# Adding scatter transfers onto rows that hold x and half the shared expert, in a Macaron block

## The chip, the cores and the metric

One core of one Trainium2 chip runs the whole program in one launch. The metric is the device time of a run in microseconds, median of several runs. The engines are named as in the profile: PE (TensorE matmuls), PEld (its weight loads), DVE (VectorE), ACT (ScalarE), POOL (GpSimd), SP (SyncE, which only issues transfers here).

## The reference

Input x has 32 x 256 = 8192 tokens of 128 features, float32. The block is feed-forward, attention, feed-forward, each on a layer norm of x:

```
x = x + 0.5 * ffn(layernorm(x))
x = x + attention(layernorm(x))        # linear attention: phi(q) (phi(k)^T v) Wo^T + bo, 16 heads of 8, per batch of 256 tokens
x = x + 0.5 * ffn(layernorm(x))
ffn(h)  = shared(h) + sum over the 2 best of 8 routed experts of score_e * down_e(silu(gate_e h) * up_e h)
shared(h) = down(silu(gate h) * up h)  # inner width 256, for the shared and for each routed expert
```

The routing (sigmoid of logits, two best of eight, scores divided by their sum) depends on the data, so tokens are sorted by expert on the chip.

## The kernel before, in words

The tokens are 16 tiles of 512; x stays in SBUF as 16 slices of 128 x 512 (four tokens a partition). The order of the work is written out by hand for each engine, with semaphores between them. The program has five parts, where f is 0 for the first feed-forward and 1 for the second.

1. Dispatch (f = 0, to about 173 us). Per tile: layer norm into `send`, transpose, router, two best experts and a place in the expert's list for each pick (`route`, DVE), the shared expert (`gate_up`, `down_shared` on PE). DVE adds half the shared expert to x in `add_shared` (line 1342). POOL scatters each tile's normalised rows, with their number and weight, into `x_rows` in HBM: `ffn_tile` (line 639), 8 indirect transfers of 128 rows per tile.
2. Slot stage f = 0 (to about 367 us). 68 slots of 256 rows of one expert (three are mixed). SP loads the rows of a slot (`load_rows`, line 508, six slots ahead), PE transposes them, gate and up are made in three fp32r matmuls each, DVE multiplies (line 1781), PE makes the down product (line 1122), DVE scales it by the row's weight into a ring of 12 result buffers (`slot_results`, lines 1791 and 1793), and POOL scatters it to `y_rows` in HBM: `slot_tile` (line 651), 2 indirect transfers of 128 rows of 512 bytes per slot. Each token has two rows there, one per pick. When a tile's slots have been sent, SP loads its 512 KB back (`load_picks`, line 528, ring of two) and DVE adds both picks to x (`add_pick`, line 1686, twice) and takes the statistics of attention's norm (`norm_stats`). Eight tiles are added inside the stage, eight later.
3. Middle (16 turns and a few on either side, to about 580 us). Turn i does attention of tile i and, one and two turns behind, routing and the shared expert of f = 1. In `attend` PE first puts the output bias into the bank (line 1196: a matmul of two rows of ones by two rows that hold bo split in two parts), then adds the four products of phi(q) (line 1199). DVE adds the bank to x (line 1858). POOL scatters rows as in the dispatch.
4. Slot stage f = 1 (to about 759 us), as the first one, with stores of finished tiles (line 532) among the loads.
5. The last loads of results, additions and stores (to 778.5 us).

POOL's own order is: all of the dispatch's transfers, then those of the 68 slots, then the same again. Nothing else of weight is on it. SP issues in one order too: ahead of a slot stage the two tables of slots, the first six slots' rows, eight paddings (line 544), then row 6 on.

Of the kernel before, what the change touches and what calls it, by code (L numbers as in the profile page):

```python
# [13 lines left out]
P = 128  # L14
# [32 lines left out]
BY_VECTOR = (2, 3)  # L47
LATE_TURN = {t: t - LATE for t in range(LATE, TILES)}
# [58 lines left out]
def macaron(nc, x_in, w_experts, router_wT, routing_bias, w_attn, bq, bv, bo, out):  # L107
# [15 lines left out]
    with ExitStack() as ctx:  # L123
# [34 lines left out]
        bo_rows = sb("bo_rows", [2, P])  # L158
        bo_hi = sb("bo_hi", [2, P], F32R)
        bo_lo = sb("bo_lo", [2, P])  # L160
        bo_first = sb("bo_first", [2, P])
        bo_parts = sb("bo_parts", [2, P], F32R)
        ones_rows = sb("ones_rows", [2, P], F32R)
# [35 lines left out]
        y_pair = sb("y_pair", [P, 2, PICKS, TT])  # L199
        nobody_pad = y_pair.rearrange("p i w n -> p (i w n)")[:, 0:(PAD_BLOCKS - ROUTED) * JS * ROW].rearrange(  # L200
# [97 lines left out]
        bq_ready, ones_ready, bo_ready = sem("bq_ready"), sem("ones_ready"), sem("bo_ready")  # L298
# [14 lines left out]
        shared_psum, shared_added = sem("shared_psum"), sem("shared_added")  # L313
# [10 lines left out]
        first_added, both_added = sem("first_added"), sem("both_added")  # L324
# [140 lines left out]
        def _(sp):  # L465
# [14 lines left out]
            sp.dma_start(bo_rows[:], bo.partition_broadcast(2)).then_inc(attn_loaded, 16)  # L480

            for e in range(1, EXPERTS):
                wait_count(sp, split_lo, 0 if e == 1 else split_expert(e - 2))
                sp.dma_start(w_raw[e % 2][:], w_experts[e, :, 0:2 * INNER]).then_inc(w_loaded[e % 2], 16)
                if e == 2:
                    sp.wait_ge(pad_ready, 1)
                    sp.dma_start(x_rows[ROUTED * region:].rearrange("(b p j) d -> p b (j d)", p=P, j=JS),
                                 nobody_pad.rearrange("p b j d -> p b (j d)")).then_inc(nobody_region, 16)

# [31 lines left out]
            def load_picks(f, t):  # L521

                n = f * tiles + t
                wait_count(sp, both_added, n - Y_RING + 1)
# [5 lines left out]
            def store_tile(t):  # L530
                sp.wait_ge(both_added, tiles + t + 1)
                sp.dma_start(out_view[t], x[:, t, :].rearrange("p (b n) -> p b n", b=2)).then_inc(stored, 16)

            for f in range(2):
                load_tables(f, 0, FIRST_SLOTS)
# [35 lines left out]
                if f == 0:  # L571
                    for t in range(len(loads), tiles):
# [13 lines left out]
        def _(pool):  # L586
# [58 lines left out]
            def slot_tile(f, s):  # L645
# [17 lines left out]
        def _(act):  # L663
# [50 lines left out]

            def send_second(f, t):
# [18 lines left out]
            def dispatch():  # L734
# [19 lines left out]
                split_high(1)  # L754
                silu_tile(f, 2)
                send_normalised(f, 4)
                high((FFN, f, 4))
                send_normalised(f, 5)
                silu_tile(f, 3)
                send_normalised(f, 6)  # L760
# [8 lines left out]
                for b in range(WRITTEN_OUT, len(BATCHES[f])):  # L769
# [7 lines left out]
                    if len(ahead) > 1:  # L777
                        high((FFN, f, ahead[1]))
                    if len(ts) > 1:
                        for c in range(HALVES):  # L780
                            silu(f * tiles + ts[1], c)
                    for t in ts:
                        if 1 <= t < EXPERTS:
                            split_high(t)
                        if t == tiles - 3:
                            act.wait_ge(attn_loaded, 80)
                            act.activation(bo_hi[:], bo_rows[:], ACT.Copy).then_inc(bo_ready, 1)
                            act.wait_ge(ones_ready, 1)
                            act.activation(ones_rows[:], ones[0:2, :], ACT.Copy).then_inc(bo_ready, 1)
# [37 lines left out]
            def slot_stage(f):  # L827
# [3 lines left out]
                for s in range(slots):  # L831
# [7 lines left out]
                    slot_silu(f, s)  # L839
                    ahead = s - NORMALISE_FROM  # L840
# [40 lines left out]
            def middle():  # L881
                for i in range(TURNS.stop):
# [3 lines left out]
                    if i + 2 < tiles:  # L886
                        high((ATTN, 1, i + 2))
                    if proj:
# [32 lines left out]
        def _(pe):  # L921
# [83 lines left out]
            def down_shared(f, t):  # L1005
# [4 lines left out]
                wait_count(pe, shared_added, n)  # L1010
# [100 lines left out]
            def slot_down(f, s):  # L1111
# [6 lines left out]
                if s == 0:  # L1118
                    pe.wait_ge(shared_added, (f + 1) * tiles)
# [69 lines left out]
            def attend(t):  # L1189
# [3 lines left out]
                pe.wait_ge(shared_added, tiles + max(0, t - LAG_G - 1))  # L1193
                if t == 0:
                    pe.wait_ge(bo_ready, 5)
                pe.matmul(att_bank[:].rearrange("p (j d) -> p j d", j=SUB), ones_rows[:],
                          bo_parts[:].unsqueeze(1).to_broadcast([2, SUB, P]), start=True, stop=False)
                for j in range(SUB):
                    last = pe.matmul(att_bank[:, j * P:(j + 1) * P], phi_q[t % 2][:, j * P:(j + 1) * P],  # L1199
                                     kvo_sb[:, j // 2, :], start=False, stop=(j == SUB - 1))  # L1200
# [43 lines left out]
        def _(dve):  # L1244
# [3 lines left out]
            def norm_stats(item):  # L1248
# [8 lines left out]
                if kind == ATTN:  # L1257
                    dve.wait_ge(both_added, t + 1)
# [420 lines left out]
            def add_pick(f, t, w):  # L1679

                n = f * tiles + t
                if w == 0:
                    dve.wait_ge(y_loaded[t % Y_RING], (n // Y_RING + 1) * 16)
                else:
# [290 lines left out]
```

## Time and profile before

| | us |
|---|---|
| median of 3 runs | 778.35 |
| lowest and highest run | 770.6, 781.48 |
| the profiled execution | 780.31 |
| its span | 778.5 |
| busy: PE, PEld | 690.4, 612.7 |
| busy: DVE, ACT, POOL | 552.3, 469.2, 535.9 |

The span is what the trace covers; the execution's own time is 1.8 us longer. Times of rows count from the start of the span. The busy time of POOL counts the generation of a transfer, not the pause behind it; that of PE counts modelled ends of pipelined matmuls.

### The profile page before, as it was taken

The numbers are of one execution on the slowest core, as the hardware profiler recorded it, in microseconds if no ns is written. First come the engines' busy times: TensorE is split into PE (matmuls) and PEld (weight loads), VectorE is DVE, ScalarE is ACT, GpSimd is POOL, SyncE is SP. The second block draws the span as 40 slices with busy tenths as digits, with TensorE's granted clock in tenths as the row PEclk, the third lists the DMA queues.
The fourth block names the chain that finished last, engine by engine and source line by source line (L and its number), as shares of the span: only waits on it lengthen the run. The fifth ranks groups of instructions, "written<-read, shape, count | busy, mean of one in ns | idle before, by whom it ended". The sixth has DMA issues, their size and how long they took to land.

```text
span 778.5 us, 17599 instructions
## 1 busy us (share of the span) xinstructions
PE 690.4 (89%) x4981; PEld 612.7 (79%) x4981; DVE 552.3 (71%) x1858; ACT 469.2 (60%) x865; POOL 535.9 (69%) x567
## 2 busy tenths in 40 slices
PE   5586867969999999899799999999989999999990
PEld 4466766859999998888566777777769999999990
DVE  6686877886555557767778888877787555567772
ACT  3334534526766776676766767676446766777760
POOL 3474777777777777777257676767777777777773
PEclk8588867989999999999999999999999999999995
DMA  9313221143354345554213211111324354467765
GB/s 279 97 52 121 78 66 49 53 124 107 101 164 132 102 130 152 151 157 137 72 55 95 70 42 43 43 45 46 87 79 122 109 169 115 136 206 227 220 202 171
DMA packets 63445, 89.65 MB, mean 115 GB/s; under 512 B 13174, under 2 KB 43768, under 8 KB 63352
## 3 DMA queue, kind: packets, MB, share of 16 engines
q1 hardware_dynamic: 46456, 53.63, 24.3%
q0 software_dynamic: 16896, 34.90, 13.3%
q8 instruction: 44, 0.72, 0.4%
q14 instruction: 49, 0.40, 0.2%
HBM read 46.36 MB, written 42.12 MB: 114 GB/s over the span
## 4 chain that ended last, share of the span: by engine, by line
PE 61%; DVE 21%; DMA 6%; issue 5%; ACT 2%; SPq 2%; POOL 1%; POOLq 0%; DVEq 0%; ACTq 0%
PE y_bank L1122 12%; PE y_bank L1016 5%; PE g_bank L924 4%; DMA y_pair<-y_rows 4%; PE g_bank L926 4%; PE u_bank L925 4%; PE u_bank L924 4%; PE u_bank L926 4%; PE g_bank L925 4%; PE g_bank L995 3%; PE u_bank L996 3%; PE tr_bank L946 2%; DVE stats L1264 2%; DVE h L1337 2%; PE y_bank L1199 2%
## 5 line engine op out<-in xcount | busy, mean ns | idle before, releaser
L639 POOL DMA_INDIRECT x_rows<-send,send_to x256 | 248.8, 972 | 144.4 <-issue 67.5
L651 POOL DMA_INDIRECT y_rows<-send,y_to x272 | 265.0, 974 | 85.2 <-issue 66.2
L1781 DVE TENSOR_TENSOR h<-silu_g,u_bank 128x512 f32<-128x512 f32 x136 | 93.2, 685 | 110.8 <-ACT silu_g L825 109.2
L800 ACT ACTIVATE slot_gu<-w_gu 128x1024 fp32r x130 | 137.7, 1060 | 40.6 <-issue 36.9
L1122 PE MATMUL y_bank<-w_dn,h 128*128 x1088 | 143.6, 275 | 0.4 <-DVE x L1342 0.4
L1122 PEld LDWEIGHTS y_bank<-w_dn,h 128*128 128x128 f32 x1088 | 132.9, 191 | 0.9 <-issue 0.8
L924 PE MATMUL g_bank<-xT_hi,slot_gu 128*128 128x256 f32 x260 | 84.8, 326 | 14.4 <-DVE xT_lo L1772 13.5
L1016 PEld LDWEIGHTS y_bank<-w_dn,h 128*128 128x128 f32 x512 | 65.3, 202 | 26.9 <-issue 26.2
L825 ACT ACTIVATE silu_g<-g_bank 128x512 f32<-128x512 f32 x136 | 78.9, 580 | 9.7 <-PE g_bank L926 9.6
L1016 PE MATMUL y_bank<-w_dn,h 128*128 128x128 f32 x512 | 66.9, 287 | 16.6 <-DVE x L1342 16.6
L699 ACT ACTIVATE silu_g<-g_bank 128x512 f32<-128x512 f32 x64 | 38.0, 596 | 72.5 <-PE u_bank L926 41.4
L925 PE MATMUL u_bank<-xT_lo,slot_gu 128*128 128x256 f32 x260 | 73.0, 281 | 0.0
L924 PE MATMUL u_bank<-xT_hi,slot_gu 128*128 128x256 f32 x260 | 73.0, 281 | 0.0
L926 PE MATMUL u_bank<-xT_hi,slot_gu 128*128 128x256 f32 x260 | 73.0, 281 | 0.0
L925 PE MATMUL g_bank<-xT_lo,slot_gu 128*128 128x256 f32 x260 | 72.9, 280 | 0.0
L926 PE MATMUL g_bank<-xT_hi,slot_gu 128*128 128x256 f32 x260 | 72.8, 280 | 0.0
L924 PEld LDWEIGHTS g_bank<-xT_hi,slot_gu 128*128 128x128 f32 x260 | 49.2, 189 | 19.9 <-DVE xT_lo L1772 18.1
L1686 DVE TENSOR_TENSOR x<-y_pair,x 128x512 f32<-128x512 f32 x64 | 43.9, 685 | 23.2 <-DMA y_pair<-y_rows 23.0
L711 ACT ACTIVATE send<-x,shift,rstd 128x128 f32<-128x128 f32 x128 | 52.5, 482 | 10.0 <-DVE shift L1304 7.9
L1793 DVE TENSOR_TENSOR send<-y_bank,send 128x256 f32<-128x256 f32 x136 | 56.8, 418 | 0.6 <-PE y_bank L1122 0.3
L925 PEld LDWEIGHTS g_bank<-xT_lo,slot_gu 128*128 128x128 f32 x260 | 49.6, 191 | 0.0
L925 PEld LDWEIGHTS u_bank<-xT_lo,slot_gu 128*128 128x128 f32 x260 | 49.2, 189 | 0.0
(258 smaller groups left out, 1484.0 us busy)
## 6 DMA issues: line engine op xcount, KB each, us to landing
send<-x_rows SPq DMA_DIRECT2D x130, 130.0 KB
y_pair<-y_rows SPq DMA_DIRECT2D x32, 512.0 KB
y_rows<-send,y_to POOLq DMA_INDIRECT x272, 2.7
x<-x_in SPq DMA_DIRECT2D x16, 256.0 KB, 7.2
x_rows<-send,send_to POOLq DMA_INDIRECT x256
out<-x SPq DMA_DIRECT2D x16, 256.0 KB
w_raw<-w_experts SPq DMA_DIRECT2D x15, 256.0 KB, 4.0
x_rows<-pad SPq DMA_DIRECT2D x16, 130.0 KB
```

The lines of the kernel that those rows point to most:

```text
L639: pool.indirect_dma_start(x_rows, bass.IndirectOffsetOnAxis(ap=send_to[b % SEND_TO_RING][:, w, k:k + 1], axis=0), send[ring_of(f, t)][:, w ...
L651: pool.indirect_dma_start(y_rows, bass.IndirectOffsetOnAxis(ap=y_to[k][:, j:j + 1], axis=0), result_rows(f, s)[:, j, :], None).then_inc(y_ ...
L711: last = act.activation(send[ring_of(f, t)][:, 0, j, 0:P], x_sub(t, j), ACT.Identity, bias=bias, scale=scale)
L800: act.activation(slot_gu[n % 2][:].rearrange("p a n -> p (a n)"), w_gu[:, bass.ds(e, 1)].rearrange("p e a n -> p (e a n)").bitcast(F32), A ...
L825: act.activation(silu_g[n % 2][:], g_bank[n % 2][:], ACT.Silu).then_inc(slot_silu_done, 1)
L924: pe.matmul(bank_ap, w_parts[0], x_parts[0], start=True, stop=False)
L925: pe.matmul(bank_ap, w_parts[0], x_parts[1], start=False, stop=False)
L926: return pe.matmul(bank_ap, w_parts[1], x_parts[0], start=False, stop=True)
L1016: last = pe.matmul(shared_bank[:, s], h[t % 2][c][:, s], w_dn[:, 0, c, :], start=(c == 0), stop=(c == HALVES - 1))
L1122: last = pe.matmul(y_bank[par][:, j * P:(j + 1) * P], h[par][0][:, c * ROWS + j * P:c * ROWS + (j + 1) * P], w_dn[:, bass.ds(e[j % len(e)] ...
L1781: dve.tensor_tensor(h[par][0][:], silu_g[par][:], u_bank[par][:], ALU.mult).then_inc(slot_h_done, 1)
L1793: dve.tensor_tensor(result_rows(f, s), y_bank[n % 2][:, 0:ROWS].rearrange("p (j d) -> p j d", j=JS), row[:, :, WEIGHT:WEIGHT + 1].to_broad ...
```

## The change

Rows of `y_rows` are no longer overwritten by the slots' results but added to. Ahead of the slots SP stores x of each tile into the rows of its first pick and half the shared expert into those of its second (`store_base`, 32 tiles x 2 transfers of 256 KB). Half the shared expert comes from ACT, out of the PSUM bank into one of two new buffers (`shared_to_half`). The scatter of line 651 gets `compute_op=ALU.add`. When a tile comes back, x is the sum of the two loaded rows: one addition in place of two, and DVE's `add_shared` is gone. The padding rows of `y_rows` are cleared once. POOL waits, ahead of slot 0 of each stage, for all 16 tiles' stores. ACT waits, ahead of a half, for the stores of the tile two before it. Attention's output bias, broadcast over the partitions (`bo_b`), is added to x by DVE (`add_bias`) between `mask_heads` and `value`, and the bias matmul with its small preparation on ACT and DVE is gone. In the first slot stage attention's statistics are taken one slot earlier.

```diff
+HALVES_AFTER = {2: (0, 1, 2), 5: (3, 4), 7: (5, 6), 8: (7,)}
@@ sync
+            def store_base(f, t):
+                sp.wait_ge(shared_halved, f * tiles + t + 1)
+                sp.dma_start(y_tiles[t][:, 0, :], x_tile(t)).then_inc(base_stored[t % 2], 16)
+                sp.dma_start(y_tiles[t][:, 1, :], shared_half[t % 2][:]).then_inc(base_stored[t % 2], 16)
             for e in range(1, EXPERTS):
                 wait_count(sp, split_lo, 0 if e == 1 else split_expert(e - 2))
                 sp.dma_start(w_raw[e % 2][:], w_experts[e, :, 0:2 * INNER]).then_inc(w_loaded[e % 2], 16)
-                if e == 2:
+                if e == 3:
                     sp.wait_ge(pad_ready, 1)
...
+                for t in HALVES_AFTER.get(e, ()):
+                    store_base(0, t)
...
             for f in range(2):
+                for t in range(HALVES_AFTER[EXPERTS - 1][-1] + 1 if f == 0 else 0, ROWS_TILE + 2 + (f == 0)):
+                    if f == 1 and t == 1:
+                        load_picks(0, tiles - 1)
+                    store_base(f, t)
                 load_tables(f, 0, FIRST_SLOTS)
...
                 for s in range(ROW_RING):
                     load_rows(f, s)
+                for t in range(ROWS_TILE + 2 + (f == 0), tiles - 1):
+                    store_base(f, t)
                 sp.wait_ge(table_step, f * TABLE_STEPS + FIRST_STEPS + 1)
                 for e in range(ROUTED):
...
+                store_base(f, tiles - 1)
                 for s in range(ROW_RING, FIRST_SLOTS):
                     load_rows(f, s)
@@ gpsimd, slot_tile
                 pool.wait_ge(y_out_done, n + 1)
+                if s == 0:
+                    pool.wait_ge(nobody_cleared, 32)
+                    for done in base_stored:
+                        pool.wait_ge(done, (f + 1) * tiles * 16)
                 for j in range(JS):
                     pool.indirect_dma_start(
                         y_rows, bass.IndirectOffsetOnAxis(ap=y_to[k][:, j:j + 1], axis=0),
-                        result_rows(f, s)[:, j, :], None).then_inc(y_sent[k], 16)
+                        result_rows(f, s)[:, j, :], None, compute_op=ALU.add).then_inc(y_sent[k], 16)
@@ scalar
+            def shared_to_half(f, t):
+                n = f * tiles + t
+                act.wait_ge(shared_psum, n + 1)
+                wait_count(act, base_stored[t % 2], n // 2 * PICKS * 16)
+                act.activation(shared_half[t % 2][:], shared_bank[:], ACT.Copy, scale=0.5).then_inc(shared_halved, 1)
@@ tensor, attend
-                pe.matmul(att_bank[:].rearrange("p (j d) -> p j d", j=SUB), ones_rows[:],
-                          bo_parts[:].unsqueeze(1).to_broadcast([2, SUB, P]), start=True, stop=False)
@@ vector
-            def add_shared(f, t):
-                dve.wait_ge(shared_psum, f * tiles + t + 1)
-                dve.scalar_tensor_tensor(out=x_tile(t), in0=shared_bank[:], scalar=0.5, in1=x_tile(t), op0=ALU.mult,
-                                         op1=ALU.add).then_inc(shared_added, 1)
-                dve.tensor_tensor(x_tile(t), y_in[t % Y_RING][:, w, :], x_tile(t), ALU.add).then_inc((first_added, both_added)[w], 1)
+                dve.tensor_tensor(x_tile(t), y_in[t % Y_RING][:, 0, :], y_in[t % Y_RING][:, 1, :], ALU.add
+                                  ).then_inc(picks_added, 1)
+            def add_bias(t):
+                dve.wait_ge(xn_done, t + 1)
+                dve.tensor_tensor(by_sub(x_tile(t)), by_sub(x_tile(t)), bo_b[:].unsqueeze(1).to_broadcast([P, SUB, P]), ALU.add
+                                  ).then_inc(bias_added, 1)
```

On DVE, at the end of the dispatch, behind the routing of the last two tiles (`pad_table` is the last piece of it, `h` the shared expert's product, `x<-y_bank` is `add_shared`, `blocks` the start of the table of slots), the order before was:

```order
L1567 CAST pad_table<-filled 1x8
L1342 SCALAR_TENSOR_TENSOR x<-y_bank,x 128x512
L1337 TENSOR_TENSOR h_0<-silu_g,u_bank 128x512
L1337 TENSOR_TENSOR h_1<-silu_g,u_bank 128x512
L1342 SCALAR_TENSOR_TENSOR x<-y_bank,x 128x512
L1569 SCALAR_TENSOR_TENSOR blocks<-filled,counting 128x80
```

In the changed kernel the same place on DVE reads:

```order
L1591 CAST pad_table<-filled 1x8
L1366 TENSOR_TENSOR h_0<-silu_g,u_bank 128x512
L1366 TENSOR_TENSOR h_1<-silu_g,u_bank 128x512
L1593 SCALAR_TENSOR_TENSOR blocks<-filled,counting 128x80
L1598 SCALAR_TENSOR_TENSOR blocks<-filled,counting 128x8
```

Both additions are gone, so that the table follows the products at once.

On PE, in a turn of the middle, where `attend` follows the second half of the next tile's projection (`attn_raw,pad`) and comes ahead of the router, before:

```order
L1186 MATMUL y_bank<-attn_raw,kv_sb 128x128 x2
L946 MATMUL tr_bank<-ident,send 128x128 x4
L1163 MATMUL g_bank<-attn_raw,pad 128x256 x2
L1196 MATMUL y_bank<-bo_parts,ones_rows 128x512
L1199 MATMUL y_bank<-kvo_sb,phi_q 128x128 x4
L967 MATMUL route_bank<-router_raw,pad 128x8 x4
```

and in the changed kernel, on PE in the same turn:

```order
L979 MATMUL tr_bank<-ident,send 128x128 x4
L1196 MATMUL g_bank<-attn_raw,pad 128x256 x2
L1228 MATMUL y_bank<-kvo_sb,phi_q 128x128 x4
L1000 MATMUL route_bank<-router_raw,pad 128x8 x4
L1202 MATMUL u_bank<-pad,attn_raw 128x512
```

The matmul of the bias is gone from each of the 16 turns; the rest keeps its order.

On SP, where the eighth padding goes out ahead of the slot stage (`x_rows<-pad`) and the seventh slot's rows follow (`send<-x_rows`), before:

```order
L544 ISA
L544 DMA x_rows<-pad 128x260
L506 TENSOR_LOAD row_table
L506 ISA x2
L508 ISA
L508 DMA send<-x_rows 128x260
```

and in the changed kernel, on SP at the same place:

```order
L561 DMA x_rows<-pad 128x260
L483 DMA y_rows<-x 128x512
L484 DMA y_rows<-shared_half 128x512
L517 TENSOR_LOAD row_table
L517 ISA x2
L519 ISA
L519 DMA send<-x_rows 128x260
```

The last tile's two stores stand between the paddings and the rows of slot 6.

## Rows read from the trace of the kernel before

**Rows 1.** Busy time of the engines in four stretches, with clock and DMA share.

```profile
core 0: us, PE busy (x) PEld busy (x) DVE busy (x) ACT busy (x) POOL busy (x), PEclk, DMA share, GB/s
300.00:320.00 20.00, 17.76 (x146) 16.93 (x147) 14.01 (x37) 13.34 (x20) 15.15 (x16) 1.00 0.51 150
500.00:520.00 20.00, 20.00 (x124) 15.05 (x124) 16.07 (x65) 14.71 (x33) 14.69 (x16) 1.00 0.14 44
640.00:660.00 20.00, 20.00 (x179) 20.00 (x178) 10.57 (x28) 12.85 (x21) 15.12 (x17) 1.00 0.45 132
700.00:720.00 20.00, 20.00 (x175) 19.80 (x174) 14.87 (x39) 14.46 (x24) 15.38 (x16) 1.00 0.76 223
```

**Rows 2.** Lines 639 and 651: GpSimd's transfers, ns min/median/max, first and last start.

```profile
L639 POOL DMA_INDIRECT x_rows<-send,send_to x256: 952/964/1369, 23.5 to 590.0; - x128
L651 POOL DMA_INDIRECT y_rows<-send,y_to x272: 952/963/1482, 201.2 to 766.0; - x136
DMA to landing us min/median/max: 2.3/2.7/4.9
```

**Rows 3.** Timeline of GpSimd: start us, us, line, operation [idle before <- releaser].

```profile
77.54 0.97 POOL L639 DMA_INDIRECT x_rows<-send,send_to  x1 [9.03 <-DVE number_weight L1438]
...
201.25 0.96 POOL L651 DMA_INDIRECT y_rows<-send,y_to  x1 [0.30 <-DVE send L1793]
...
374.25 0.97 POOL L651 DMA_INDIRECT y_rows<-send,y_to  x1 [0.31 <-issue]
...
591.30 0.96 POOL L651 DMA_INDIRECT y_rows<-send,y_to  x1 [0.30 <-issue]
...
766.01 0.96 POOL L651 DMA_INDIRECT y_rows<-send,y_to  x1 [0.30 <-issue]
```

**Rows 4.** Timeline of TensorE in one turn of the middle.

```profile
445.76 1.03 PE L1163 MATMUL g_bank<-attn_raw,pad 128*128 128x256 f32 x4
446.72 0.49 PE L1196 MATMUL y_bank<-bo_parts,ones_rows 2*128 2x512 f32 x1
447.14 1.16 PE L1199 MATMUL y_bank<-kvo_sb,phi_q 128*128 128x128 f32 x8
```

**Rows 5.** Timeline of ScalarE in the same turn.

```profile
445.08 0.60 ACT L699 ACTIVATE silu_g<-g_bank 128x512 f32<-128x512 f32 x1 [0.87 <-PE u_bank L996]
```

**Rows 6.** Timeline of VectorE where the first slot stage begins.

```profile
168.09 0.69 DVE L1342 SCALAR_TENSOR_TENSOR x<-y_bank,x 128x512 f32<-128x512 f32 x1 [1.02 <-PE y_bank L1016]
...
173.42 0.42 DVE L1772 TENSOR_TENSOR xT_lo<-tr_bank,xT_hi 128x256 fp32r<-128x256 f32 x1
...
179.25 0.69 DVE L1342 SCALAR_TENSOR_TENSOR x<-y_bank,x 128x512 f32<-128x512 f32 x1 [1.64 <-PE y_bank L1016]
```

**Rows 7.** Timeline of TensorE where the first slot stage begins.

```profile
173.89 0.58 PE L924 MATMUL g_bank<-xT_hi,slot_gu 128*128 128x256 f32 x1 [5.40 <-DVE xT_lo L1772]
```

**Rows 8.** Timeline of SyncE's transfers ahead of both slot stages.

```profile
162.70 6.41 SPq L508 DMA_DIRECT2D send<-x_rows  x6
...
577.75 8.73 SPq L544 DMA_DIRECT2D x_rows<-pad  x8
```

**Rows 9.** Timeline of VectorE at one of stage 0's loads of results.

```profile
298.54 0.69 DVE L1686 TENSOR_TENSOR x<-y_pair,x 128x512 f32<-128x512 f32 x1 [1.77 <-DMA y_pair<-y_rows]
...
300.55 0.68 DVE L1686 TENSOR_TENSOR x<-y_pair,x 128x512 f32<-128x512 f32 x1
```

**Rows 10.** Waits from 280 to 366 us: us in total, times, longest.

```profile
DVE x L1686 <- DMA y_pair<-y_rows: 11.9, 8, 2.3
```

**Rows 11.** Timeline of VectorE at the end.

```profile
767.56 1.42 DVE L1686 TENSOR_TENSOR x<-y_pair,x 128x512 f32<-128x512 f32 x2 [7.01 <-DMA y_pair<-y_rows]
...
774.49 1.42 DVE L1686 TENSOR_TENSOR x<-y_pair,x 128x512 f32<-128x512 f32 x2 [0.33 <-DMA y_pair<-y_rows]
```

**Rows 12.** DMA queues: packets, MB, share of 16 engines.

```profile
q1 hardware_dynamic: 46456, 53.63, 24.3%
q0 software_dynamic: 16896, 34.90, 13.3%
```

More of the change, by code:

```diff
@@ L199, in macaron @@
         y_pair = sb("y_pair", [P, 2, PICKS, TT])
+        shared_half = two("shared_half", [P, TT])
         nobody_pad = y_pair.rearrange("p i w n -> p (i w n)")[:, 0:(PAD_BLOCKS - ROUTED) * JS * ROW].rearrange(
@@ L488, in _ @@
                                  nobody_pad.rearrange("p b j d -> p b (j d)")).then_inc(nobody_region, 16)
+                    for b, n in ((0, ROUTED), (ROUTED, PAD_BLOCKS - ROUTED)):
+                        sp.dma_start(y_rows[nobody + b * ROWS:nobody + (b + n) * ROWS].rearrange("(p k) d -> p k d", p=P),
+                                     pad.rearrange("p e j d -> p (e j) d")[:, 0:n * JS, 0:P]).then_inc(nobody_cleared, 16)
+                if e == 2:
+                    sp.wait_ge(x_rest, 16 * (tiles - 4))
+                for t in HALVES_AFTER.get(e, ()):
+                    store_base(0, t)
             def load_tables(f, first, last):
@@ L571, in _ @@
                 if f == 0:
-                    for t in range(len(loads), tiles):
+                    for t in range(len(loads), tiles - 1):
                         load_picks(f, t)
@@ L784, in dispatch @@
                             split_high(t)
[L785 to L789, printed above, removed]
                     if b + 2 < len(BATCHES[f]):
@@ L839, in slot_stage @@
                     slot_silu(f, s)
+                    if s == 0:
+                        shared_to_half(f, tiles - 1)
                     ahead = s - NORMALISE_FROM
@@ L887, in middle @@
                         high((ATTN, 1, i + 2))
+                    if 0 <= i - LAG_G - 2 < tiles - 1:
+                        shared_to_half(1, i - LAG_G - 2)
                     if proj:
@@ L1118, in slot_down @@
                 if s == 0:
-                    pe.wait_ge(shared_added, (f + 1) * tiles)
+                    pe.wait_ge(shared_halved, (f + 1) * tiles)
                 for j in range(JS):
@@ L1192, in attend @@
                 wait_count(pe, x_attended, t)
[L1193 to L1197 removed]
+                pe.wait_ge(shared_halved, tiles + max(0, t - LAG_G - 1))
                 for j in range(SUB):
                     last = pe.matmul(att_bank[:, j * P:(j + 1) * P], phi_q[t % 2][:, j * P:(j + 1) * P],
[L1200 removed]
+                                     kvo_sb[:, j // 2, :], start=True, stop=True)
                 last.then_inc(att_psum, 1)
@@ L1713, in dispatch @@
                 norm(3)
-                add_shared(f, 0)
                 multiply_tile(f, 2)
                 norm(4)
-                add_shared(f, 1)
                 low((FFN, f, 4))
@@ L1721, in dispatch @@
                 padding_constants()
-                add_shared(f, 2)
                 for t in range(1, 4):
@@ L1805, in slot_stage @@
                     table_piece(f, (s, THEN))
-                    if s == 0:
-                        add_shared(f, tiles - 1)
                     table_piece(f, (s, BEHIND))
@@ L1890, in middle @@
                         mask_heads(i)
+                        add_bias(i)
                     if 0 < i + 1 < tiles:
                         value(i + 1, 0)
-                    for t in late:
-                        add_pick(0, t, 0)
                     if g:
@@ L1928, in middle @@
                         route(1, i - LAG_T, MASK_STEP, RECIP_STEP)
-                    if 0 <= i - LAG_G - 1 < tiles - 1:
-                        add_shared(1, i - LAG_G - 1)
                     if g and i - LAG_G == tiles - 1:
@@ L1939, in _ @@
             for t in range(tiles):
-                for w in range(PICKS):
-                    if first_add(1, t) + w >= slots:
-                        add_pick(1, t, w)
+                if first_add(1, t) >= slots:
+                    add_picks(1, t)
 _OUT = ((32, 256, 128), "float32")
```

58 lines of the change are left out of this document (23 added, 35 removed).

## The prediction

> **What bounds the kernel now.** I read the windows first. In both slot stages PE is full or nearly so: 20.00 of 20 us at 640 and 700, 17.76 at 300; in the middle, at 500, it is 20.00 as well, with DVE at 16.07 and ACT at 14.71 [rows 1]. That looks like a PE kernel, and DVE's additions like work beside the path. But POOL shows 15.1 to 15.4 of 20 in every slot window, with 16 or 17 transfers, and that is a full engine too: a transfer takes 0.96 us and 0.30 us pass before the next [rows 2, 3], 1.26 us together, and 16 of them fill 20 us. From 77.54, after a wait of 9.03 us for DVE's routing, to 201.25 POOL makes 96 transfers of the dispatch (123.7 us, 1.29 each), from 201.25 to 374.25 the 136 of stage 0 (1.28 a pitch), and from 591.30 to 766.01 the 136 of stage 1 (1.29) [rows 3]. PE's 68 slots are done some 8 us earlier each time. So the end of the program hangs on POOL: last transfer at 766.01, 0.96 for it, landing 2.7 [rows 2], the last load of results, the last two pairs of additions from 774.49 on [rows 11], the last store. Stage 1 is POOL's from its first transfer on; in it nothing that DVE, ACT or PE saves can count, only what lets POOL start earlier or go faster. After stage 0 POOL has slack: it stands still from 375 until the middle has routed a tile, so stage 0 and the middle are paced by PE, with the waits of rows 6, 7 and 9.
>
> **The change part by part.** I sum against the profiled execution, 780.3 us; the median of the three runs, 778.35, is 2.0 below it.
>
> *The bias matmul goes (16 turns).* In a turn that is PE's from end to end the bias starts at 446.72 and the first product behind it at 447.14 [rows 4]: 0.42 us. 16 x 0.42 = 6.7 us off PE in the middle. Bounds: 16 x the matmul's own 0.49 = 7.9, and 0 if another engine takes the turn over. What comes in its place: an addition on DVE of the size of line 1342 (0.69 us [rows 6]), while add_shared (0.69) leaves each turn, and in the first eight turns one of two pick additions (0.68 [rows 9]) as well. DVE is not longer in any turn. ACT gets one copy of 128x512 out of PSUM, like the silu of 0.60 us [rows 5]; it stands just ahead of that silu, which waited 0.87 us for PE. It fits, with 0.3 us to spare. I take -6.7.
>
> *add_shared leaves the dispatch and the first slot.* The first slot's gate matmul starts at 173.89, after PE stood still for 5.40 us for DVE's xT_lo at 173.42 [rows 6, 7]. The slot's rows were asked for at 162.70 [rows 8], so that is about 5 us later than its input allows. DVE was late because it had two add_shared to do, the second after a wait of 1.02 us for PE, and then the table; and at 179.25 a third, after 1.64 us. Those alone are 0.69 + 1.02 + 0.69 + 1.64 + 0.69 = 4.7 us of DVE's row, and some more was saved in the pairs of tiles before. The row request itself waits for POOL's transfers of the dispatch and does not move. Bounds: 0 and the whole 5.4 + 1.6 + 0.7 = 7.7. I take -5.0.
>
> *POOL's start in the dispatch.* POOL's last gap is the 9.03 us until 77.54 [rows 3], for routing of tiles 4 and 5, and DVE has up to three add_shared less ahead of it; against that six stores now stand between SP's loads of the experts. Bounds +1 and -3 x 0.69 = -2.1; I take -1.0.
>
> *The pick additions.* In stage 0 DVE waits for loads of results, 11.9 us in eight waits [rows 10], for example 1.77 us until 298.54 [rows 9]. The load keeps its place on SP and its 512 KB, so the wait stays; what goes is the second addition, 0.68 us at 300.55, and DVE has idle time behind it, in the two slots that follow. Against that the load lands later, as the adding transfers need more of the DMA engines. Bounds -8 x 0.68 = -5.4 and +8 x 1 us; I take +2. POOL's own lag now counts more, since stage 0 starts 5 us earlier and POOL doesn't: +1.
>
> *x and halves stored.* 64 transfers of 256 KB, 16.8 MB, and 2 MB of padding rows once. SP was idle in those times. At stage 1 it comes last: the eight paddings run from 577.75 to 586.5 [rows 8], then the last tile's two stores are issued, and POOL, which now waits for them, would want to start its slots at 591.30 [rows 3]. They have 4 to 5 us, and transfers here land in 2.3 to 4.9 us [rows 2]. 0 to +3; I take 0. Behind this wait stand all 136 transfers, but POOL's dispatch is what ends last ahead of it.
>
> *The end.* One addition of 0.7 us less behind the last load, and an adding transfer lands perhaps 1 us later (it must read what it adds to): +0.3.
>
> *The transfer itself.* Its 272 instances [rows 2] are the term with the largest lever, and no row shows one that adds. The nearest row is line 639's: the same number of rows, each 8 bytes longer, and the same 0.96 us. So the bytes cost nothing, and what costs is the instruction and its 128 rows. Adding changes neither. Bounds: 0, and +0.96 us if everything were done twice. By the row that it is nearest to, I take 0 for the forecast, and price the rest as a rival.
>
> The Trainium skill speaks against this value. "GPSIMD Engine Reference", section "4. When to use GPSIMD", says that one core writes the read descriptors of such a transfer and another the write descriptors; and "Collectives: The Full Stack", part 3, "Why ReduceScatter is half of AllGather", says that an addition in the DMA needs two reads for each piece and so two read descriptors. 
>
> **The rivals.**
>
> *POOL's transfer gets longer (slower than before).* Place: line 651's instruction, on POOL. Each d us more costs 136 x d at stage 1 in full. In stage 0 POOL's lag is taken up by the 12 result buffers (12 slots, 30 us, of which some 17 are used at its start), so about half of 136 x d. With d = 0.2: 27 + 14 = 41, and 770 + 41 = 811 us; with d = 0.1, 790; with d = 0.48 (half as long again) 868. It decides from d of 0.12, where 24 us more make it slower by 2%. For it: POOL has no slack at all [rows 3], and an adding transfer must name its target as a source too. Against it: 639 and 651 take the same time, so most of it looks like a fixed price.
>
> *The DMA engines fill up.* q0's 16,896 packets took 13.3% of 16 engines' span, 98 ns each, 32 to a transfer: 0.2 us on every engine, of a pitch of 1.29. If adding breaks a transfer into its 128 rows at q1's mean of 65 ns (24.3% of 16 x 778.5 over 46,456 packets) [rows 12], it is 0.5 us, and with two reads up to 1.0: 0.25 to 0.6 more of the engines' time, where at 700 us 0.76 are in use already [rows 1]. The last 80 us of stage 1 would stretch by up to a third, say 15 us, and the loads of stage 0 land 1.5 us later eight times: 770 + 15 + 12 = 797.
>
> *The gain is larger.* The waits of rows 10 go with the additions, since DVE catches up (11.9 us), or the dispatch gains by more than its end: 770 - 10 = 760.
>
> **How the numbers follow.** Forecast, POOL's pitch unchanged: 0.46, own range 762 to 780. POOL longer: 0.32. DMA full: 0.10. Larger gain: 0.12. About 2% is what a measurement of this kernel can tell from no change: 763 to 794. The forecast lies inside, and a sixth of the POOL case does (d under 0.12): same 0.51. The rest of POOL's and most of the DMA case are slower: 0.37. Faster 0.12. The range: down to 760, where half of the larger gain is left out (0.06), and up to 830, where d is 0.3 (0.13 left out).
>
> **What would show it.** Right: line 651 still at 0.96 us with 1.26 to 1.29 between starts; 136 transfers in about 174 us; a turn of the middle shorter by 0.4 us; the first gate matmul of stage 0 near 169; POOL's first slot transfer of stage 1 right behind its last of line 639's kind. Wrong: line 651 above 1.0 us and POOL's last transfer late by 136 times that, whatever DVE and PE show; or the DMA share above 0.95 with DVE waiting for y_pair in stage 1, where it did not; or a gap on POOL ahead of either stage's first slot, which would be the stores' wait.

## The result and the profile after

The changed kernel takes **914.46 us** (median of 4 runs, 911.93 to 916.03) against 777.37 us for the kernel before on the same chip (4 runs): a ratio of 1.177, 95% interval 1.171 to 1.182. It is slower, by 137 us. The profiled execution took 911.93 us, with a span of 910.1.

GpSimd first, since the forecast hung on its transfers. The view of the tensor y_rows, with line 673's transfers (line 651 of before, [rows 2]), gives count, ns min/median/max, first and last start:

```profile
L673 POOL DMA_INDIRECT y_rows<-send,y_to x272: 1552/1552/2064, 197.9 to 897.5; - x136
its engine sat idle before it (us, times) until:
  issue: 76.2, 250
  DMA y_rows<-shared_half: 4.3, 1
...
DMA to landing us min/median/max: 3.2/3.4/11.6
```

The same 272 instructions take 1.55 us instead of 0.96. The pause between two is still 0.30 (76.2 us in 250), and 1.86 us apart they fill POOL. The median landing has gone from 2.7 to 3.4 us; the maximum of 11.6 is that of a clearing of the padding rows, and line 673's own is 6.7. GpSimd's timeline (start, us, line, [idle before]) at the ends of the stages, to be laid beside [rows 3]:

```profile
21.68 1.29 POOL L657 DMA_INDIRECT x_rows<-send,send_to  x1 [12.92 <-DVE send L1473]
...
197.94 1.62 POOL L673 DMA_INDIRECT y_rows<-send,y_to  x1 [0.30 <-DVE y_to L1801]
...
452.31 0.99 POOL L657 DMA_INDIRECT x_rows<-send,send_to  x1 [0.30 <-issue]
...
646.64 1.61 POOL L673 DMA_INDIRECT y_rows<-send,y_to  x1 [4.30 <-DMA y_rows<-shared_half]
...
897.54 1.55 POOL L673 DMA_INDIRECT y_rows<-send,y_to  x1 [0.30 <-issue]
```

From first to last start the 136 transfers of stage 1 take 250.9 us, against 174.7 in [rows 3]; stage 0's take 254.4 from their first to the middle's first. The very first adding transfer already took 1.62 us, with only plain transfers ahead of it in its queue, so the price is not one of adding transfers that pile up. And the middle's first transfer starts 0.30 us behind the last of stage 0: POOL has no standstill left. Busy time of the engines in four stretches, beside [rows 1]:

```profile
core 0: us, PE busy (x) PEld busy (x) DVE busy (x) ACT busy (x) POOL busy (x), PEclk, DMA share, GB/s
500.00:520.00 20.00, 20.00 (x126) 15.63 (x125) 17.81 (x69) 15.03 (x32) 14.42 (x16) 1.00 0.28 97
700.00:720.00 20.00, 20.00 (x178) 20.00 (x176) 11.20 (x31) 13.71 (x22) 16.65 (x12) 1.00 0.60 87
780.00:800.00 20.00, 19.80 (x171) 19.40 (x170) 12.14 (x32) 14.64 (x24) 16.65 (x12) 1.00 0.95 208
880.00:900.00 20.00, 0.00 (x0) 0.00 (x0) 1.39 (x2) 0.00 (x0) 16.05 (x11) 0.50 0.68 125
```

12 transfers fit into 20 us where 16 or 17 did. From 880 to 900 TensorE is done and POOL alone works on. At 700 TensorE is still at full pace, because it can run ahead of POOL by the twelve result buffers: in stage 1 VectorE first finds them full at 719.53, and TensorE stands only after that, for 31.3 us until 768.49, waiting for the rows of a slot. SyncE issues nothing from 727.28 to 763.40; the load of results that it then issues waits for POOL's transfers, and the rows' loads come behind it. Where the slot stages wait (engine line waited for: us in total, times, longest):

```profile
DVE y_to L1801 <- DMA y_rows<-send,y_to: 89.3, 41, 3.9
...
ACT xT_hi L837 <- PE route_bank L1109: 74.7, 56, 32.4
...
PE g_bank L957 <- DVE xT_lo L1782: 49.3, 32, 9.9
```

The first row is the twelve result buffers run full: VectorE may not write the next result until the transfer of twelve slots earlier has landed, so it stands, and the other engines behind it. 77.0 of the 89.3 us are in stage 0, where the buffers are full from 218.94 on. Queues (packets, MB, share of 16 engines), beside [rows 12]:

```profile
q0 software_dynamic: 47360, 34.90, 27.2%
q1 hardware_dynamic: 59684, 72.45, 26.3%
```

At 32 packets for each of the 256 transfers of the dispatch, the 272 adding ones have 144 each: one for each of the 128 rows and 16 besides. In DMA time q0 went from 0.20 us of every engine per transfer to (0.272 x 910.1 - 256 x 0.196) / 272 = 0.73.

### The profile page after: what moved, and what is told of

Same layout as the page of the kernel before. It is cut to its first block and busy times, and to the rows that moved or that the text cites. A ratio compares the mean times of both kernels' runs of the same rounds, so it can differ in the third digit from the quotient of the medians.

```text
span 910.1 us, 17660 instructions
## 1 busy us (share of the span) xinstructions
PE 707.9 (78%) x4965; PEld 631.1 (69%) x4965; DVE 524.9 (58%) x1807; ACT 487.8 (54%) x895; POOL 694.6 (76%) x567
## 5 line engine op out<-in xcount | busy, mean ns | idle before, releaser
L673 POOL DMA_INDIRECT y_rows<-send,y_to x272 | 424.2, 1560 | 86.9 <-issue 76.2
L1155 PE MATMUL y_bank<-w_dn,h 128*128 x1088 | 150.7, 284 | 0.1
L1155 PEld LDWEIGHTS y_bank<-w_dn,h 128*128 128x128 f32 x1088 | 140.2, 200 | 0.7 <-issue 0.5
L957 PE MATMUL g_bank<-xT_hi,slot_gu 128*128 128x256 f32 x260 | 88.5, 340 | 49.5 <-DVE xT_lo L1782 49.3
L957 PEld LDWEIGHTS g_bank<-xT_hi,slot_gu 128*128 128x128 f32 x260 | 52.1, 200 | 58.6 <-DVE xT_lo L1782 58.0
L1801 DVE CAST y_to<-send 128x2 int32<-128x2 f32 x136 | 26.4, 194 | 89.3 <-DMA y_rows<-send,y_to 89.3
L959 PE MATMUL u_bank<-xT_hi,slot_gu 128*128 128x256 f32 x260 | 75.5, 290 | 0.0
L959 PE MATMUL g_bank<-xT_hi,slot_gu 128*128 128x256 f32 x260 | 75.2, 289 | 0.0
L957 PE MATMUL u_bank<-xT_hi,slot_gu 128*128 128x256 f32 x260 | 75.2, 289 | 0.0
L1049 PEld LDWEIGHTS y_bank<-w_dn,h 128*128 128x128 f32 x512 | 62.5, 193 | 8.5 <-issue 7.2
L837 ACT ACTIVATE xT_hi<-route_bank 128x256 fp32r<-128x256 f32 x62 | 23.8, 384 | 75.0 <-PE route_bank L1109 74.7
L1049 PE MATMUL y_bank<-w_dn,h 128*128 128x128 f32 x512 | 62.7, 276 | 0.0
L837 ACT ACTIVATE xT_hi<-tr_bank 128x256 fp32r<-128x256 f32 x68 | 26.0, 383 | 64.4 <-PE tr_bank L1109 64.1
```

The costliest lines, as they stand in the source:

```text
L673: pool.indirect_dma_start(y_rows, bass.IndirectOffsetOnAxis(ap=y_to[k][:, j:j + 1], axis=0), result_rows(f, s)[:, j, :], None, compute_op= ...
L957: pe.matmul(bank_ap, w_parts[0], x_parts[0], start=True, stop=False)
L959: return pe.matmul(bank_ap, w_parts[1], x_parts[0], start=False, stop=True)
L1049: last = pe.matmul(shared_bank[:, s], h[t % 2][c][:, s], w_dn[:, 0, c, :], start=(c == 0), stop=(c == HALVES - 1))
L1155: last = pe.matmul(y_bank[par][:, j * P:(j + 1) * P], h[par][0][:, c * ROWS + j * P:c * ROWS + (j + 1) * P], w_dn[:, bass.ds(e[j % len(e)] ...
```

## The experiments

"The overwriting transfer" below is the transfer without the addition. Where a kernel leaves a part of the computation out, its expectation says so, or the diff shows it.

### The changed kernel without the addition

```diff
-result_rows(f, s)[:, j, :], None, compute_op=ALU.add)
+result_rows(f, s)[:, j, :], None)
```

Its output lacks x and the shared expert.

> The changed kernel with line 673's transfers overwriting again (so x and half the shared expert are missing from the output); all stores, waits, the smaller work of DVE and PE stay. Theory 1, the 0.60 us more that POOL takes for each adding transfer (1.552 against 0.958 us) is the whole loss: the line goes back to 0.96 us and 1.26 between starts, and the time to 763 to 771 us, below the kernel before, since the first slot starts 7.3 us earlier and a turn of the middle is 0.6 us shorter. Theory 2, the base stores and the waits for them are a large part: above 800 us.

Measured: 766.43 us (765.87 to 768.21), ratio to before 0.984, interval 0.982 to 0.987. GpSimd's timeline:

```profile
200.94 0.97 POOL L673 DMA_INDIRECT y_rows<-send,y_to  x1 [0.31 <-issue]
...
387.93 0.97 POOL L657 DMA_INDIRECT x_rows<-send,send_to  x1 [13.27 <-DVE send L1473]
...
583.17 0.96 POOL L673 DMA_INDIRECT y_rows<-send,y_to  x1 [4.00 <-DVE send L1803]
...
754.51 0.96 POOL L673 DMA_INDIRECT y_rows<-send,y_to  x1 [0.30 <-issue]
```

One argument of one call is worth 148 us. Everything else in the change together, its 64 stores included, saves 11.7. The wait of 4.00 us at 583.17 is put down to VectorE, but slot 0's result was there before it. SyncE's and VectorE's timeline just ahead:

```profile
578.34 0.45 SPq L483 DMA_DIRECT2D y_rows<-x  x1
578.60 0.42 DVE L1803 TENSOR_TENSOR send<-y_bank,send 128x256 f32<-128x256 f32 x1
578.84 0.46 SPq L484 DMA_DIRECT2D y_rows<-shared_half  x1
```

VectorE's line 1803 is slot 0's result, ready at 579.02; POOL's list of the middle ended at 579.17. POOL's transfer also waits for all 16 tiles' stores, and the last of these was issued only at 578.84. So the stores' wait costs POOL 3.7 us here, the 4.00 less the usual pause of 0.30.

### The addition alone, in the kernel before

```diff
+sp.dma_start(y_rows[...], pad[...]).then_inc(cleared_rows, 16)
-result_rows(f, s)[:, j, :], None).then_inc(y_sent[k], 16)
+result_rows(f, s)[:, j, :], None, compute_op=ALU.add).then_inc(y_sent[k], 16)
```

The result tensor is cleared in the dispatch, once; stage 1 adds to what stage 0 left, so its output is another.

> The kernel before with nothing changed but the compute_op of line 651's transfers (and y_rows cleared once in the dispatch; the second stage adds to the first's results, so the output is another). Theory 1: 136 transfers at a pitch of 1.86 in each stage, stage 0's overhang stops the middle from starting: 905 to 925 us. Theory 2: below 850.

Measured: 956.35 us, ratio 1.229; line 658 takes 1552 ns here as well. The size was missed by some 30 to 50 us. The transfers are as dear as expected, but the clearing wasn't free: SyncE issues it from 62.27 on, ahead of the experts' weights, whose next load goes out at 98.17 instead of 63.75, and POOL stands still for 46.46 us before 114.56, waiting for routing (in before its longest wait there is 9.03). POOL's first slot transfer comes at 237.21 instead of 201.25.

```profile
237.21 1.62 POOL L658 DMA_INDIRECT y_rows<-send,y_to  x1 [0.31 <-issue]
...
492.79 0.99 POOL L644 DMA_INDIRECT x_rows<-send,send_to  x1 [0.30 <-issue]
...
688.60 1.61 POOL L658 DMA_INDIRECT y_rows<-send,y_to  x1 [0.30 <-issue]
```

Without those 36.0 us it is 920. In stage 1, first to last start, the addition costs 78.4 us here (253.1 against before's 174.7) and 79.6 in the changed kernel (250.9 against 171.3 overwriting): nearly the same beside before's VectorE as beside the changed one.

### The addition in one stage only

```diff
+compute_op=ALU.add if f == 0 else ALU.bypass
```

and the same with `f == 1`. The stage that overwrites leaves out x and the shared expert.

> The changed kernel adding in slot stage 0 only; stage 1 overwrites (its output lacks x and the shared expert). The prediction's rule, half of POOL's lag is taken up in stage 0: 0.5 x 136 x 0.60 = 41 us above the overwriting kernel, 808. Theory 1 with the middle's first transfer queued behind the stage's last: POOL's 81 us less the 18 us it stood still before the middle, about 62 above it, 829 (822 to 836).

> The changed kernel adding in slot stage 1 only; stage 0 overwrites (x and the shared expert are missing there). Both rules: all of 136 x 0.60 = 81 us above the overwriting kernel, 844 to 850 us. If the overwriting kernel lost anything that the adding one hides, less.

Measured: 833.93 us (831.51 to 836.35) with the addition in stage 0, 849.25 (847.10 to 851.41) in stage 1; that is +67.5 and +82.8 on the 766.4 without. The sum, 766.4 + 67.5 + 82.8 = 916.7, is the changed kernel's 914.5 to 0.3%: the two stages' costs add up. In the timeline of the first of them POOL goes straight from stage 0 into the middle:

```profile
198.03 1.61 POOL L673 DMA_INDIRECT y_rows<-send,y_to  x1 [0.30 <-issue]
...
453.40 0.99 POOL L657 DMA_INDIRECT x_rows<-send,send_to  x1 [0.31 <-issue]
```

136 x 0.59 = 80 us, less the 13.3 us for which POOL stood still ahead of the middle in the overwriting kernel, is 67: what was measured. "Half of it" (40) falls.

### What in the transfer costs: half the rows

```diff
-ap=y_to[k][:, j:j + 1]
+ap=y_to[k][0:P // 2, j:j + 1]
```

64 rows per transfer instead of 128 (so half the bytes too), adding and overwriting; half the results are left out.

> The changed kernel with 64 of the 128 rows in each of line 673's adding transfers (half of the results are left out). If the 0.60 us more of an adding transfer are the price of its rows' further descriptors, 4.7 ns a row, half of it goes, and the duration is that of the overwriting transfer of 64 rows plus 0.30. If they are the price of another path in the instruction, fixed, it is plus 0.60.

> As the one before, overwriting: 64 rows in each transfer (half of the results, x and the shared expert are left out). Gives the fixed part and the part per row of the plain transfer: 0.96 us if it is all fixed, 0.48 if it is all rows; with it the adding transfer's two parts.

Measured: 868.26 us adding and 768.08 overwriting, one run each. Line 673's instructions (ns min/median/max) in the adding one:

```profile
L673 POOL DMA_INDIRECT y_rows<-send,y_to x272: 1390/1403/1871, 196.1 to 854.2; - x136
```

and in the overwriting one:

```profile
L673 POOL DMA_INDIRECT y_rows<-send,y_to x272: 891/902/1394, 200.9 to 753.5; - x136
```

Overwriting: 0.963 and 0.902 us, so 0.061 for 64 rows and 0.84 that doesn't depend on them. Adding: 1.552 and 1.403, so 0.149 for 64 rows and 1.25 fixed. Of the 0.59 us more, 0.41 is in the fixed part and 0.18 in the rows, if both are straight lines through two points each. Neither a pure price per row nor a pure fixed one holds; the larger part is fixed. q0 had 29,952 packets: 80 to a transfer, again one for each row and 16.

### The bias by VectorE alone, in the kernel before

```diff
-pe.matmul(att_bank[...], ones_rows[:], bo_parts[...], start=True, stop=False)
+dve.tensor_tensor(x_tile(t), x_tile(t), bo_b[...], ALU.add)
```

> The kernel before with the other part of the change alone: attention's output bias added by DVE, the bias matmul gone; nothing adds in a transfer. By the prediction's term: 16 x 0.42 = 6.7 us less, 770 to 771 by the median of before (777.4), with a turn of the middle at 12.2 us. If the changed kernel's shorter turn (12.02 against 12.64) is all the bias's: 10 us less. If DVE, which here loses no addition in its place, paces the turn: no gain.

Measured: 777.09 us (12 runs) against 775.83 (17), ratio 1.001, interval 0.998 to 1.004. No gain. Both sides are seen in TensorE's timeline of the middle: its turn stays at about 12.5 us until attention's ninth tile (before: 12.64), then one takes 16.12 (before: 13.35), and only from there on the turns are 12.02.

```profile
454.82 1.05 PE L1185 MATMUL y_bank<-kvo_sb,phi_q 128*128 128x128 f32 x8
...
470.94 1.05 PE L1185 MATMUL y_bank<-kvo_sb,phi_q 128*128 128x128 f32 x8
...
482.96 1.05 PE L1185 MATMUL y_bank<-kvo_sb,phi_q 128*128 128x128 f32 x8
```

And the waits from 400 to 560 us say who took over:

```profile
ACT send L706 <- DVE shift L1306: 7.8, 8, 1.1
...
PE g_bank L985 <- DVE h L1323: 4.4, 3, 2.0
```

In before these two are 0.9 us in 2 waits and 2.4 in 2. In the three turns up to 454.82 VectorE is busy for 34.69 of 37.36 us, and it has two pick additions in each; the last of them starts at 457.11. From 482.96 on, with the shared addition and the bias but no picks, it is busy for 21.11 of 24.04, and the turn is as short as in the changed kernel. So the turns with two pick additions are the ones where the bias has no room. The shared additions alone do not take its place: the first complete version below has none of them in the middle, but two pick additions, and its turns are 12.55, 12.75 and then 16.68 us.

The balance is best drawn against the run with the last halves late (below), whose middle is before's: from attention's first tile to its last 185.5 us here, 185.2 there. Before's own trace has 188.5, but of an execution of 780.31 us, 4.5 above the median of the 17 runs of before given here.

### The changed kernel, overwriting, with the bias matmul back

```diff
-dve.tensor_tensor(x_tile(t), x_tile(t), bo_b[...], ALU.add)
+pe.matmul(att_bank[...], ones_rows[:], bo_parts[...], start=True, stop=False)
```

On top of the first experiment's edit, so x and the shared expert are left out here too.

> k1_overwrite (the changed kernel with the overwriting transfer, 766.4 us) with one part undone: the bias comes by the matmul again and VectorE's addition of it is gone. It tells what the bias is worth where VectorE has been relieved of the shared additions. Theory (the gain of 0.42 us a turn is only there where VectorE has room for the bias): turns of 12.64 us instead of 12.02, 766.4 + 5.8 = 772 us, range 770 to 774. Rival (the bias is worth nothing here either, as in k3, and k1's 11.7 us are all the shared expert's): 766 to 768.

Measured: 769.76 us (10 runs), ratio 0.993, interval 0.990 to 0.996, against 0.984 (0.982 to 0.987) for the same kernel with the bias by VectorE. By medians 3.3 us, by ratios 6: the turns are back at 12.64 us, as the theory had it, and the time is a little below its range. So moving the bias is worth something where a tile has one pick addition, and nothing in the kernel before, where it has two.

In this run the profile puts POOL's wait ahead of stage 1 down to the stores themselves, in a kernel that overwrites:

```profile
581.87 0.95 POOL L678 DMA_INDIRECT y_rows<-send,y_to  x1 [3.83 <-DMA y_rows<-shared_half]
```

### Two complete versions that keep the useful parts

The first keeps all of the change but the addition: the shared expert's half goes through a tensor of its own and is added by VectorE within the slots.

```diff
+sp.dma_start(shared_rows[f * tiles + t], shared_half[t % 2][:])
+sp.dma_start(shared_half[t % 2][:], shared_rows[f * tiles + t])
+dve.tensor_tensor(x_tile(t), x_tile(t), shared_half[t % 2][:], ALU.add)
-result_rows(f, s)[:, j, :], None, compute_op=ALU.add)
+result_rows(f, s)[:, j, :], None)
```

> The changed kernel with the overwriting transfer. ACT still makes half the shared expert, but it alone is stored, to a tensor of its own (one store of 256 KB a tile, not two), and comes back by one load a tile in every third slot from slot 18 on; VectorE adds it to x there, and the two picks in two additions, as before. No x is stored, no padding rows are cleared and POOL waits for no store. The output is complete. Theory (POOL's adding is all that was lost, and VectorE is idle for over 40% of the slots, 22 us busy of 40): k1's 766.4 us, plus 3 to 4 us because the first eight turns of the middle have two pick additions beside the bias again, as in k3, plus 0.7 at the end: 770 to 771, range 767 to 774, some 0.8% below before. Rival (the 32 additions and loads get in the way in the slots, by SP's order or VectorE's): 777 or more, no gain over before, with a wait for shared_half or for the load of rows in the slot windows.

Measured: 797.78 us (6 runs), ratio 1.026, interval 1.022 to 1.030. The theory fell; the rival's sign was right. Stage 0 from POOL's first slot transfer to the middle's first takes 201.4 us (overwriting kernel: 187.0), the middle 204.3 (195.2), stage 1 180.8 (171.3). In the middle the longer turns are those with two pick additions beside the bias, named above. The waits from 270 to 330 us:

```profile
PE g_bank L962 <- DVE xT_lo L1794: 11.7, 5, 5.8
...
DVE x L1712 <- DMA y_pair<-y_rows: 7.7, 3, 4.7
```

In the overwriting kernel TensorE's wait there is 4.8 us and the longest 2.1. VectorE stood at the head of its queue for one load of results for 4.67 us (until 283.59), with the next slot's work behind it. This load was issued only at 279.77, when VectorE had stood since 278.92, and VectorE went on 3.8 us later. Ahead of it SyncE issued nothing for 4.6 us, so this load did not queue behind added transfers; it waits for POOL to have sent the tile's slots. What made the stages as a whole longer, the additions on VectorE or the added transfers, no run separates. But "VectorE is idle for over 40% of the slots" was no licence: where its work ahead of a slot came late, as here, TensorE waited.

The second takes only the last three shared additions of stage 0's dispatch off VectorE, in the kernel before, without any new transfer:

```diff
+act.activation(late_half[t - (tiles - 3)], shared_bank[:], ACT.Copy, scale=0.5)
+dve.tensor_tensor(x_tile(t), late_half[t - (tiles - 3)], x_tile(t), ALU.add)
```

> The kernel before, complete output, with one small part of the change's idea and none of its transfers: in stage 0 the shared additions of the last three tiles (13 to 15) leave the end of the dispatch. ACT copies half the shared expert of these tiles from PSUM to the (still unused) y_pair buffers, and VectorE adds them to x in slots 4, 6 and 8. Theory (the change's useful part is mostly that VectorE is free at the end of the dispatch, 7.3 us at the first gate matmul and 3 us more by the time the middle starts): 5 to 6 us off before, 770 to 772 where before is 776, ratio 0.992 to 0.994, and the first slot's gate matmul near 169 to 170. Rival (stage 0 is POOL's by then, whose first slot transfer does not move, so nothing is gained): 775 to 777.

Measured: 774.00 us (12 runs) against 776.53 (23), ratio 0.997, interval 0.994 to 0.9999: 2.5 us, about half of what was expected, and only just clear of nothing. TensorE's first gate matmul:

```profile
171.98 0.58 PE L936 MATMUL g_bank<-xT_hi,slot_gu 128*128 128x256 f32 x1 [4.04 <-DVE xT_lo L1789]
```

It is 1.9 us earlier than in [rows 7], not 4 to 5. Single executions differ here, though: the run below has the same additions taken out of the dispatch and starts it at 169.59, 4.3 earlier. The middle's first transfer comes at 389.16 instead of 392.95. The last run adds to this the bias by VectorE for tiles 9 to 15:

```diff
+by_pe = t < 9
+if t >= 9: dve.tensor_tensor(x_tile(t), x_tile(t), bo_b[...], ALU.add)
```

> k10_last_halves_late, complete output, and attention's bias from tile 9 on added by VectorE, by the matmul for tiles 0 to 8. In k3's middle VectorE was short of time only in the turns with pick additions (tiles 0 to 8 of attention); behind them its turns were 12.02 us against 12.64. Theory: 7 turns by 0.62 = 4.3 us off k10, some of it taken back at the end of the middle: k10 minus 3 to 4 us, about 767, ratio to before 0.988. Rival (the bias is worth nothing wherever VectorE still has the shared additions): the same as k10.

Measured: 774.49 us (12 runs), ratio 0.998, interval 0.995 to 1.001. From 478.68 on its turns are 12.02 us, as expected, and its profiled span is 769.7 us against 771.9 for the one before; but by the medians of 12 runs each nothing is gained, 774.49 against 774.00. The two cannot be told apart. The fastest complete version of this study is the one before this, 0.3% ahead of the kernel before, at the edge of what these runs can tell.

## Why the prediction was wrong

**The step that failed** is "The transfer itself": "Adding changes neither. ... By the row that it is nearest to, I take 0". It measured +0.59 us on each of 272 transfers, inside the bounds given (0 to 0.96) and far from the end taken. The argument was at fault, not the reading. Line 639's row differs from 651's by 8 bytes a row, and so tells what these cost; it doesn't add either, and says nothing about adding. With no row on either side of the question, both ends were open, on a term that counts 136 to 272 times. "What costs is the instruction and its 128 rows" also was half wrong: 64 rows fewer save only 0.06 of 0.96 us.

**The rival had the mechanism, its price a second error.** "POOL's transfer gets longer" held in place and in sign; 0.59 lies far beyond the 0.12 from which it was to decide. By its own formula d = 0.59 gives 136 x 0.59 = 80 for stage 1 and 40 for stage 0: 770 + 120 = 890, still 24 too low. The step that failed there is "POOL's lag is taken up by the 12 result buffers". Buffers delay a lag; they don't remove it. The middle needs POOL for its own dispatch, so the whole of stage 0's list must be done first, and only POOL's standstill before the middle, 17.7 us less the usual 0.3, absorbs some; the run with the addition in stage 0 alone shows it, at +67.5 us instead of 40. From 197.94 to 452.01 the list takes 254.1 us against 174.0: +80.1, less 17.4 is 62.7. The start was 3.3 earlier, which leaves the 59.4 that the middle was late (452.31 against 392.95). The range reached to d = 0.3, where the bound was 0.96.

**The Trainium skill's warning was in the right direction.** The prediction named it by "GPSIMD Engine Reference", section "4. When to use GPSIMD", and "Collectives: The Full Stack", part 3, "Why ReduceScatter is half of AllGather": an addition needs two reads; from that it worked out that one core's list of descriptors would double. The trace agrees in sign (1.55 against 0.96 us). It doesn't show a doubling of the instruction, which is 1.61 times as long, and the half-row runs put most of the growth into the part that doesn't depend on rows; the rule alone doesn't explain that.

**Point by point.**
- *Bias matmul, -6.7.* Turn 12.02 us instead of 12.64: 0.62 each, more than the 0.42 of [rows 4]. But alone it gained nothing, since VectorE took over in the turns with two pick additions; with one of them gone it is worth 3 to 6 us. The clause "DVE is not longer in any turn" holds for the whole change and not for this part of it.
- *add_shared off the first slot, -5.0.* The first gate matmul starts at 166.54 against 173.89. 1.8 us of it is a start that was earlier in this run (first transfer at 21.68, against 23.51); 5.5 remain. Right in size, but less sure than it looks. The run with the bias alone, whose first transfer is at 23.50, has it at 171.36, 2.5 us earlier, with add_shared in its place. VectorE's preparation of the bias rows, gone there, doesn't explain it: put back into the overwriting kernel it changes nothing (144.7 us from first transfer to first gate matmul, against 145.0). What does is open.
- *POOL's start in the dispatch, -1.0.* From first transfer to first slot transfer 176.3 us against 177.7: -1.5. The overwriting kernel, with the same dispatch, has 177.4, so part of it is spread.
- *Stores' wait, 0 (0 to +3).* The wait came, 4.30 us, 4.0 more than the usual pause, and it is there at normal speed too: 3.7 us more in the overwriting kernel, where it stands ahead of all of stage 1. The prediction's reason for 0, that POOL's dispatch ends last ahead of the slots, held in before and no longer did: POOL's list of the middle ended at 579.17 in the overwriting kernel against 591.0, while the last store still came behind the paddings.
- *The end, +0.3.* 11.0 us behind the last transfer against 11.5: -0.5.
- *All of it without the addition, -9.4.* Measured -11.7. The sum is near partly by luck. By the two traces, whose first transfers start together, POOL is 0.3 us earlier at stage 0, then gains 4.7 in it and 3.1 in the middle with the stores' 3.7 inside, so 6.8 without them. Stage 1 is 3.4 us shorter (171.3 against 174.7), which the prediction had ruled out ("in it nothing that DVE, ACT or PE saves can count"): in before three of POOL's pauses there are longer than 0.4 us, in the overwriting kernel none. The stores' wait that it put at 0 and the gain that it put at 0 cancel.
- *DMA engines fill up.* The share rose to 0.95 at 780 and the engine time per transfer from 0.20 to 0.73 us, 0.53 more where the rival named 0.25 to 0.6. But 250.9 us for stage 1 are 135 steps of 1.86, the transfer and its pause and no more: full DMA engines cost POOL nothing here. VectorE did wait longer for loads of results, 41.6 us in nine waits against 23.0 in eleven over the whole kernel, but the loads themselves wait for POOL's late transfers: in the longest, 13.2 us until 897.83, the load was issued only at 893.52.

## What to carry to other kernels

An operation added to an instruction on the engine that ends last is priced before anything else; if no row shows it, a row that differs in something else is no evidence, and a term that counts hundreds of times keeps both its ends in the range. A ring of buffers between two engines postpones a lag, and only a standstill of the slower one absorbs it: look for what that engine has to do next. Work moved to an engine that is "40% idle" need not be free: its idle time can lie inside a chain that each step repeats. And where an instruction waits for several things, the one that the profile names is compared with its own end: here it was long done, and the wait was another's.

## What was not expected of the hardware

- An indirect transfer by GpSimd of 128 rows of 512 bytes takes 0.96 us overwriting and 1.55 us adding; with 64 rows 0.90 and 1.40. It makes one packet for each row and 16 more where it adds (144 and 80), 32 where it doesn't, with 128 rows or 64.
- One of the first instructions of VectorE, the same 128x4 operation, takes 0.19 to 0.39 us in some profiled executions and 3.91 to 4.21 in others, and the first transfer starts at 20.3 to 21.7 us in the former and at 23.3 to 23.8 in the latter. Profiles are best laid over each other at that transfer. VectorE's timeline of before:

```profile
4.49 3.99 DVE L1285 TENSOR_SCALAR half_var<-stats 128x4 f32<-128x4 f32 x1
```

and of the changed kernel, the same instruction:

```profile
4.34 0.28 DVE L1314 TENSOR_SCALAR half_var<-stats 128x4 f32<-128x4 f32 x1
```
